# The product with v cut into quarters that skip the masked part, and TensorE's products of the high part put ahead of the wait for the low part

## The reference

```
def local_attention(q, k, v):                       # WINDOW = 128, 8 heads of 64, 32 windows per batch row
    bk, bv = look_around(bk), look_around(bv)       # keys and values of the window before, and of this one
    sim = einsum('bhwid,bhwjd->bhwij', bq, bk)      # 128 queries x 256 keys
    mask = (i < j) | (i > j + WINDOW) | (j == -1)
    attn = softmax(where(mask, -max, sim))
    out = einsum('bhwij,bhwjd->bhwid', attn, bv)
...
x = x + o @ wo
h = layernorm(shift_token(x)) * lg + lb
a, g = split(h @ w1 + b1);  x = x + (a * gelu(g)) @ w2 + b2
```

## Time and profile before

| | us |
|---|---|
| median of 3 runs | 2906.41 (2905.05 to 2906.92) |
| the profiled execution | 2907.57 |
| its span | 2905.6 |
| TensorE busy, matmuls | 2801.5 (96%) |
| VectorE busy | 2240.0 (77%) |
| ScalarE busy | 2231.9 (77%) |
| GpSimd busy | 1618.5 (56%) |
| granted TensorE clock, mean | 0.986 |

### The profile page before, as it was taken

The page is one execution under the profiler, slowest core; times in us unless marked ns, Lnnn a source line. Parts: engine busy times, 40 slices in busy tenths (PEclk is TensorE's granted clock), DMA queues, the critical chain, the costliest instruction groups (busy, mean ns, idle before and its releaser), DMA issues.

```text
span 2905.6 us, 67281 instructions
## 1 busy us (share of the span) xinstructions
PE 2801.5 (96%) x23076; PEld 2538.9 (87%) x23076; DVE 2240.0 (77%) x6331; ACT 2231.9 (77%) x5429; POOL 1618.5 (56%) x1652
## 2 busy tenths in 40 slices
PE   7999948999999999999999999999999999999998
PEld 6878837899989998999899899999999999999988
DVE  3979978887888788778878677777777777777773
ACT  4979956877877787787778677777777777777784
POOL 2323226656666665666666555666666666666653
PEclk9999968999999999999999999999999999999999
DMA  3252111211111111111111213111111111111111
GB/s 99 64 183 78 39 58 50 60 45 56 56 53 47 56 52 47 54 56 55 48 54 41 81 56 104 49 49 49 48 45 46 49 49 49 47 47 48 43 43 35
DMA packets 211301, 166.21 MB, mean 57 GB/s; under 512 B 21522, under 2 KB 206612, under 8 KB 209940
## 3 DMA queue, kind: packets, MB, share of 16 engines
q1 hardware_dynamic: 139284, 127.82, 14.5%
q10 hardware_dynamic: 71680, 34.10, 4.0%
HBM read 110.89 MB, written 42.58 MB: 53 GB/s over the span
## 4 chain that ended last, share of the span: by engine, by line
PE 85%; DVE 8%; issue 2%; ACT 2%; DMA 1%; POOL 1%; SPq 1%; DVEq 0%; ACTq 0%; POOLq 0%
PE ps L387 47%; PE ps L361 10%; PE ps L471 8%; PE ps L457 7%; PE ps L445 6%; DVE Sm L1074 3%; PE ps L430 3%; DVE oTl L1093 1%; PE ps L407 1%; DVE Ar L1045 1%; PE ps L496 1%; DMA oF<-ro_scratch 1%; PE ps L533 1%; PE ps L348 1%; PE ps L532 1%
## 5 line engine op out<-in xcount | busy, mean ns | idle before, releaser
L730 ACT ACTIVATE Sm<-Sm,nb 128x256 f32<-128x256 f32 (+1 forms) x1024 | 502.6, 494 | 1.4 <-DVE nb L1074 0.7
L1074 DVE CUSTOM_DVE_ANT_0 Sm<-ps,mask,sc 128x256 f32<-128x256 f32 (+1 forms) x1024 | 420.5, 476 | 94.3 <-PE ps L445 85.7
L1215 POOL TENSOR_TENSOR rs<-rs,mhalf 128x8 f32<-128x8 f32 x256 | 421.6, 1647 | 14.1
L1303 POOL TENSOR_TENSOR uTl<-Gl,uTh 128x512 fp32r<-128x512 f32 (+1 forms) x192 | 212.5, 1107 | 361.4 <-ACT uTh L798 225.9
L387 PE MATMUL ps<-zTh,W1h 128*128 128x256 f32 (+1 forms) x1408 | 406.4, 289 | 0.0
L387 PE MATMUL ps<-zTl,W1h 128*128 128x256 f32 (+1 forms) x1408 | 397.6, 282 | 0.0
L387 PE MATMUL ps<-zTh,W1l 128*128 128x256 f32 (+1 forms) x1408 | 395.3, 281 | 0.0
L1142 DVE SCALAR_TENSOR_TENSOR Gl<-ps,vecs,Gl 128x256 f32<-128x256 f32 (+1 forms) x384 | 172.1, 476 | 286.1 <-PE ps L387 249.2
L710 ACT ACTIVATE sq<-ps 128x512 f32<-128x512 f32 x256 | 151.6, 592 | 304.0 <-PE ps L387 300.2
L387 PE MATMUL ps<-WQh,hTh 128*128 128x512 f32 x768 | 341.3, 444 | 4.1 <-DVE hTl L1029 4.1
L737 ACT ACTIVATE PT<-ps 128x512 f32<-128x512 f32 (+1 forms) x512 | 269.1, 589 | 62.6 <-PE ps L457 62.5
(11 more groups left out here) (186 smaller groups left out, 8677.7 us busy)
## 6 DMA issues: line engine op xcount, KB each, us to landing
oF<-ro_scratch ACTq DMA_DIRECT2D x256, 128.0 KB, 3.0
tb<-tab SPq DMA_DIRECT2D x128, 128.0 KB, 2.3
xc<-x SPq DMA_DIRECT2D x32, 256.0 KB, 3.0
rwkv_scratch<-rw SPq DMA_DIRECT2D x32, 256.0 KB, 2.7
rk<-rwkv_scratch SPq DMA_DIRECT2D x64, 128.0 KB, 2.3
xin<-x SPq DMA_DIRECT2D x64, 128.0 KB, 2.3
x_scratch<-x SPq DMA_DIRECT2D x64, 128.0 KB, 1.7
y_scratch<-os SPq DMA_DIRECT2D x64, 128.0 KB, 4.2
```

The source lines that it names most:

```text
L730: act.activation(Sm[:, h, c0:c1_], Sm[:, h, c0:c1_], ACT.Exp, bias=nb[:, h:h + 1], scale=-1.0, accum_out=sm[:, n % 2, h:h + 1]).then_inc(S ...
L1074: dve.tensor_tensor_reduce(Sm[:, h, c0:c1_], PS[:, bank["scores", n, q, h % 2], (h // 2 % 2) * 256 + c0:(h // 2 % 2) * 256 + c1_], mask[:, ...
L1215: return pool.tensor_tensor(ap, ap, mhalf[:, 0:ap.shape[-1]], ALU.pow)
L1303: pool.tensor_tensor(uT[1][:, j, :], Gl[:, g, :], uT[0][:, j, :].bitcast(F32), ALU.subtract).then_inc(S["ul"], 1)
```

## The change

There are two parts.

One: `pv` is cut into quarters of the array, 64 keys by 64 columns. In a first round, for each pair of heads, keys 0 to 63 of this window and keys 64 to 127 of the window before are each multiplied with all 128 queries (four products, one in each quarter of the array). In a second round keys 0 to 63 of the window before meet only queries 0 to 63, and keys 64 to 127 of this window only queries 64 to 127, accumulating (four products of 64 queries). In the first window of a batch row, which has none before it, both rounds are replaced by one round on this window's keys. The upper and the lower half of the array's rows write different PSUM banks, so `pv` now has two banks in the ring. ScalarE copies one of them to SBUF (`o_out`, new, with the tile oS), at the head of its step; VectorE adds the other (a new instruction in `o_norm`), and the multiplication by oF now reads SBUF.

Two: `mm3` gives way to `high_first` in `pre_mm`, `qkv`, `wo_mm`, `mlp` and `w2_mm`. TensorE waits for the high part, does all products that need only it, then waits for the low part and does the rest. The number of products is unchanged.

```
-                for c in (2 * q, 2 * q + 1):
-                    for s in sides:
-                        v = n % NV if s == n % 2 else (n - 1) % NV
-                        for par in range(2):
-                            ins = pe.matmul(PS[64 * par:64 * par + 64, k, c * 128:(c + 1) * 128], vv[:, v, 2 * c + par, :],
-                                            PT[:, 2 * c + par, s * 128:(s + 1) * 128],
+                here, prev = n % 2, 1 - n % 2
+                for r in range(2):
+                    w.wait_ge(*read_out(former["pv", n, r]))
+                for c in (2 * q, 2 * q + 1):
+                    for r in range(2):
+                        rows = slice(64 * r, 64 * r + 64)
+                        side, v = (prev, n - 1) if r and not first_win(n) else (here, n)
+                        for par in range(2):
+                            ins = pe.matmul(PS[64 * par:64 * par + 64, bank["pv", n, r], c * 128:(c + 1) * 128],
+                                            vv[rows, v % NV, 2 * c + par, :],
+                                            PT[rows, 2 * c + par, side * 128:(side + 1) * 128], start=True,
+                                            stop=first_win(n))
+                    if first_win(n):
+                        continue
+                    for r in range(2):
+                        rows = slice(64 * r, 64 * r + 64)
+                        side, v = (here, n) if r else (prev, n - 1)
+                        for par in range(2):
+                            ins = pe.matmul(PS[64 * par:64 * par + 64, bank["pv", n, r],
+                                               c * 128 + 64 * r:c * 128 + 64 * r + 64],
+                                            vv[rows, v % NV, 2 * c + par, :],
+                                            PT[rows, 2 * c + par, side * 128 + 64 * r:side * 128 + 64 * r + 64],
+                                            start=False, stop=True)
...
+            def o_out(n):
+                w.wait_ge(S["p6"], 2 * n + 2)
+                w.wait_ge(S["on"], n)
+                act.activation(flat(oS[:, :, :]), PS[:, bank["pv", n, 0], :], ACT.Copy).then_inc(S["oX"], 1)
...
+                w.wait_ge(S["oX"], n + 1)
+                dve.tensor_tensor(flat(oS[:, :, :]), PS[:, bank["pv", n, 1], :], flat(oS[:, :, :]),
+                                  ALU.add).then_inc(S["osum"], 1)
+                w.wait_ge(S["osum"], n + 1)
                 w.wait_ge(S[f"lro{n % 2}"], 32 * (n // 2 + 1))
-                dve.tensor_tensor(o, PS[:, bank["pv", n], :], o, ALU.mult).then_inc(S["on"], 1)
+                dve.tensor_tensor(o, flat(oS[:, :, :]), o, ALU.mult).then_inc(S["on"], 1)
...
+            def high_first(dst, ks, D, W, lows, weights_left=False):
+                for k in ks:
+                    for b in (0, 1):
+                        product(0, b, k, start=k == ks[0] and b == 0, stop=False)
+                lows()
+                for k in ks:
+                    ins = product(1, 0, k, start=False, stop=k == ks[-1])
+                return ins
...
             def w2_mm(n):
-                w.wait_ge(S["ul"], 3 * (n // 2) + 3)
-                w.wait_ge(S["ut"], n // 2 + 1)
+                w.wait_ge(S["uh"], 4 * (n // 2) + 3)
```

More of the change, by code:

```diff
@@ L100, in psum_order2 @@
     if live(6):
-        yield "pv", t - 6
+        yield "pv", t - 6, 0
+        yield "pv", t - 6, 1
     if live(7):
@@ L388, in mm3, with product @@
                 return ins
+            def high_first(dst, ks, D, W, lows, weights_left=False):
+                def product(a, b, k, **flags):
+                    if weights_left:
+                        return pe.matmul(dst, W(b, k), D(a, k), **flags)
+                    return pe.matmul(dst, D(a, k), W(b, k), **flags)
+                for k in ks:
[5 more added lines that the diff above has]
+                return ins
             def reloaded(n, what, value):
@@ L395, in pre_mm @@
                 k = bank["pre", n]
-                w.wait_ge(S["nTl"], n + 1)
+                w.wait_ge(S["nTh"], n + 1)
                 w.wait_ge(*read_out(former["pre", n]))
-                for c in range(2):
-                    ins = mm3(PS[:, k, 0:256], lambda a: nT[a][:, c, :], lambda a: Wp[a][:, c, :], c == 0, c == 1)
-                ins.then_inc(S["p0"], 1)
+                high_first(PS[:, k, 0:256], (0, 1), lambda a, c: nT[a][:, c, :], lambda a, c: Wp[a][:, c, :],
+                           lambda: w.wait_ge(S["nTl"], n + 1)).then_inc(S["p0"], 1)
             def turn_h(n):
@@ L416, in qkv @@
                 reloaded(n, "q", 32)
-                for c in range(2):
-                    ins = mm3(PS[:, k, :], lambda a: hT[a][:, c, 1 - c:129 - c],
-                              lambda a: WQ[a][:, c, i * 512:(i + 1) * 512], c == 0, c == 1)
-                ins.then_inc(S["p2"], 1)
+                high_first(PS[:, k, :], (0, 1), lambda a, c: hT[a][:, c, 1 - c:129 - c],
+                           lambda a, c: WQ[a][:, c, i * 512:(i + 1) * 512],
+                           lambda: w.wait_ge(S["hTl"], n + 1)).then_inc(S["p2"], 1)
             def turn_qk(n, i):
@@ L483, in wo_mm @@
                 k = bank["wo", n]
-                w.wait_ge(S["oTl"], n + 1)
+                w.wait_ge(S["oTh"], n + 1)
                 w.wait_ge(*read_out(former["wo", n]))
                 reloaded(n, "o", 32)
-                for c in range(4):
-                    ins = mm3(PS[:, k, 0:256], lambda a: oT[a][:, c, :], lambda a: WO[a][:, c, :], c == 0, c == 3)
-                ins.then_inc(S["p8"], 1)
+                high_first(PS[:, k, 0:256], (0, 1, 2, 3), lambda a, c: oT[a][:, c, :], lambda a, c: WO[a][:, c, :],
+                           lambda: w.wait_ge(S["oTl"], n + 1)).then_inc(S["p8"], 1)
             def turn_z(n):
@@ L507, in mlp, with low @@
                     ups = [(0, 512, 128)]
[L508 removed]
+                w.wait_ge(S["zTh"], 2 * m + 2)
                 reloaded(2 * m, "1", 32)
+                def low():
+                    w.wait_ge(S["zTl"], 2 * m + 2)
                 w.wait_ge(*read_out(former["gate", m, part]))
                 for o, wcol, v in gates:
[L512 to L515 removed]
+                    high_first(PS[0:v, kg, o * 256:o * 256 + 256], (0, 1), lambda a, c: zT[a][:, c, :],
+                               lambda a, c: W1[a][:, c, wcol:wcol + v], low, True).then_inc(S["p11"], 1)
                 w.wait_ge(*read_out(former["up", m, part]))
                 for o, wcol, v in ups:
[L518 to L521 removed]
+                    high_first(PS[0:v, ka, o * 256:o * 256 + 256], (0, 1), lambda a, c: zT[a][:, c, :],
+                               lambda a, c: W1[a][:, c, wcol:wcol + v], low, True).then_inc(S["p11"], 1)
             def w2_mm(n):
@@ L525, in w2_mm, with low @@
                 cl = slice(n % 2 * 128, n % 2 * 128 + 128)
-                w.wait_ge(S["ul"], 3 * (n // 2) + 3)
-                w.wait_ge(S["ut"], n // 2 + 1)
+                w.wait_ge(S["uh"], 4 * (n // 2) + 3)
                 w.wait_ge(*read_out(former["w2", n]))
                 reloaded(n, "2", 64)
-                for j in range(5):
-                    mm3(PS[:, k, 0:256], lambda a: uT[a][:, j, cl], lambda a: W2[a][:, j, :], j == 0, False)
-                pe.matmul(PS[:, k, 0:256], uT[0][:, 5, cl], W2[0][:, 5, :], start=False, stop=False)
-                pe.matmul(PS[:, k, 0:256], uT[0][:, 5, cl], W2[1][:, 5, :], start=False,
-                          stop=True).then_inc(S["p12"], 1)
+                def low():
+                    w.wait_ge(S["ut"], n // 2 + 1)
+                    pe.matmul(PS[:, k, 0:256], uT[0][:, 5, cl], W2[0][:, 5, :], start=False, stop=False)
+                    pe.matmul(PS[:, k, 0:256], uT[0][:, 5, cl], W2[1][:, 5, :], start=False, stop=False)
+                    w.wait_ge(S["ul"], 3 * (n // 2) + 3)
+                high_first(PS[:, k, 0:256], (0, 1, 2, 3, 4), lambda a, j: uT[a][:, j, cl],
+                           lambda a, j: W2[a][:, j, :], low).then_inc(S["p12"], 1)
             for t in range(STEPS2):
```

20 lines of the change are left out of this document (5 added, 15 removed).

## The result

The changed kernel takes 2855.99 us in the median of 4 runs (2855.33 to 2858.49), the kernel before on the same chip 2906.66 (2905.05 to 2907.33): a ratio of 0.983, 95% interval 0.981 to 0.984. The time forecast was 2856. That it came out so close is luck: two errors of 7 us or so cancel, part one brings less than the sum had, part two more. The experiments separate them.

The account below looks back on a forecast made before the run. TensorE's work was taken to bound the kernel. The terms -52 (quarters), +3 (rope wait), +1 (unseen waits) and -3.5 (high part first) were summed as -51, from 2906.4 to 2907.6 us down to 2856, range 2845 to 2912.

Parts of the forecast that it names:

- the term of 52: Product with v on quarters: 0.416 us less TensorE work in each of 124 windows, 52 us off.
- The rope wait: Output product in layer one's w2 steps waits for the rope of q: at most 0.1 x 31 = 3 us lost.
- I take 1 for unseen small waits: Allowance in the sum for small TensorE waits not worked out: 1 us lost.
- for oTl what is gained (0.69) is paid back by the new addition: Output product's wait for its low part: starting with the high part gains 0.69 us, VectorE's new addition cancels it.
- all 11: Upper bound for high part first: all waits for uTl (7.1 us) and oTl (4.3 us) vanish, 11 us off.
- The cover of ScalarE and VectorE: Their idle waits in MLP and w2 steps hide 61 us more ScalarE and 88 us more VectorE work.
- The bound of 10 us: Forecast wrong if TensorE's waits for ScalarE's exponentials, gelu or copies add up to 10 us or more.
- the first rival: Other engines eat half the gain: each of 62 MLP steps loses 0.4 us, +25, so 2881; chance 0.15.
- The others that I worked out in the same way keep more: Other waits for PSUM banks in the ring keep more room than the output product's 0.1 us before the rope.
- Short matmuls that are not shorter: Rival: in the product with v a round of 64 queries takes 0.109 us, nothing saved, 2904; chance 0.09.
- The estimate of 1.6 us per window: Product with v: about 60 cycles' overhead per matmul, 64 one after another, would give 1.6 us per window, 2889.
- Two parts at a time: Rival: only two array parts work together in the product with v, 3022, or 3120 if queue-paced; chance of both 0.14.

Follow-up runs that it names:

- e1: Kernel before with part one alone (product with v on quarters; all other products in the old order, waiting for the low part at once): 2866.66 us, ratio 0.987.
- e3: Kernel after, with the second round of the product with v streaming all 128 queries instead of the valid 64: 2899.05 us, ratio 0.997 to the kernel before.
- e4: Kernel after without the second round of the product with v, so a quarter of its valid weights is missing: 2824.32 us, ratio 0.971 to the kernel before.
- e5: Kernel after with ScalarE's new copy done twice, once into an unused tile: 2870.11 us, ratio 0.988 to the kernel before.
- e6: Kernel after with VectorE's new addition done twice, once into an unused tile: 2878.35 us, ratio 0.990 to the kernel before.
- e8: Kernel after with ScalarE's new copy behind the four exponentials of its step, no longer ahead of them: 2911.30 us, ratio 1.0015 to the kernel before.
- e7: Kernel after with the same matmuls ordered quarter by quarter, each quarter's long then short product: 2872.02 us, ratio 0.988 to the kernel before.
- e9: Kernel after with the transposes of the exponentials split into two row halves of the array: 2841.85 us, ratio 0.978 to the kernel before.

## Why the prediction was right, and where it was not

*Quarters work side by side: right.* 0.34 us per head pair where 0.332 was worked out; the product 1.50 us, 0.399 less and not 0.416. A short round takes 0.055 (2123.72 - 2123.61 for two), just under the 0.057 chosen. 124 x 0.399 = 49.5 for the term of 52. (The sum itself adds up to 51.5 and was written as 51.)

*Part one's small terms: too small.* With 3 and 1 for waits its sum was -48; e1 has -41. The rope wait is as forecast: in layer one's w2 steps the product takes 1.58 and not 1.50, 0.08 each, 2.1 us in the 26 of the steady stretch. What failed is the step "I take 1 for unseen small waits": I checked the steady state alone. While the pipeline fills, TensorE waits for the exponentials, and the copy stands ahead of them: windows 0 to 8 lose 3.0 us in e1 instead of gaining 8 x 0.4 = 3.2 (they lose 1.8 with part two), and e3 puts 3.5 us on the copy and the addition as a whole.

*High part first: the mechanism right, the size too small by three.* 3.5 forecast, 12 measured (9.0 by the spans). The three waits for uTl gave 3.1 of the 3.3 that I had for them. The failed step is "for oTl what is gained (0.69) is paid back by the new addition". The addition did make it later, by 1.2 us in all (4.3 before, 5.5 in e1), but a product that begins with its high part hides not only the low part's subtraction but as much of the wait as its first eight products last: with part two 0.9 is left (and 0.3 for oTh). The waits for hTl (4.0 to 2.8) and nTl (4.4 to 3.5) I hadn't priced at all. They stand in the same list as the rows I took, so "all 11" was no upper bound: the low parts' waits in the kernel before are 7.1 + 4.4 + 4.3 + 4.1 = 19.9 us. The measured 11 to 12 lie at its edge.

*The cover of ScalarE and VectorE: right for this change, and thin.* VectorE's busy time grew by the 85 us worked out, ScalarE's by 52 and not 61; the steady stretches show no loss in e3. The bound of 10 us for the first rival was nearly met by the exponentials alone (9.6 us), and passed if the waits for ScalarE's high parts are counted (uTh 4.0, hTh 2.8, oTh 0.3: 16.7 in all). These stand in the fill and the drain, not in the MLP steps that the rival named, and the high parts' took the place of longer waits for low parts: the sign was badly chosen, and the time, the table and e3 decide against the rival. e4, e5, e6 and e8 show that it was near: 0.69 more on VectorE costs 22 us, a copy 2 us later costs 55. "The others that I worked out in the same way keep more" was true, but only by 0.44 us for the bank that VectorE's `x2_out` frees and by some 0.3 for the bank that ScalarE's first copy frees in layer two (0.41 less the signal's 0.1). Both come ahead of the idle times that I counted as cover, so these did not protect them.

*The rivals.* Short matmuls that are not shorter: out (e3 against the kernel after). The estimate of 1.6 us per window that stands beside it is out too: the whole product takes 1.50 us, and a short round takes half of a long one. Two parts at a time: out, by the counts in fours, and e7 shows that TensorE looks past twelve matmuls, so that the "three products" of that rival were much too few.

## What to carry to other kernels

Before work is moved from the bound engine to two others, list for every wait between them how much earlier its release comes than its use, in us: here 1.6 became 0.5, the change was free in the steady stretches, and the next 0.7 cost 22 us. The busy share doesn't show such waits: it stayed over 99% in layer two of e5, where each w2 step lost 0.33 us. Price waits at the program's start and end apart from the steady state: both errors of size here were made there, and "high part first" gained only there. When TensorE works in parts of the array, put blocks with the same split next to each other; each change between whole array and row halves cost about 0.1 us in e9.

## What the runs showed of the hardware

- Matmuls for different quarters start 7 ns apart in the kernel after. In e7 they start 13 ns apart and out of the program's order: four long ones within 0.05 us, and the 13th and 14th of the program before the 3rd. Grouping by quarter still costs 10% (1.64 against 1.50 us).
- A float32 matmul of 64 rows and 64 columns with 64 streamed columns takes half of one with 128 (0.11 against 0.22 us per eight on four quarters); no fixed cost per matmul is seen at 64 matmuls in 1.50 us.
- Float32 transposes follow each other in 0.107 us on the whole array; in two halves of rows a pair of 64 columns each follows in 0.06.
- One VectorE multiplication of 128x512 took 1.24 us in e8 and 0.69 in the kernel after. Two wide operations of GpSimd ran beside it, one of them slowed from 0.74 to 1.18 us; no run tests the cause.
